# An expert layer that sends its results back to token order, instead of gathering them afterwards

## The reference

```python
x = x + gnn0(layernorm(x), adj)     # three gated graph layers (GRU)
x = x + ffn0(layernorm(x))          # 8 experts, the best 2 per token, relu
x = x + gnn1(layernorm(x), adj)     # relational graph layer, gated
x = x + ffn1(layernorm(x))          # norm again, 8 experts, best 2, gelu
```

## Time and profile before

| what | us |
|---|---|
| run, median of three | 1913.77 |
| profiled execution: span from first to last instruction | 1878.7 |
| TensorE, VectorE, ScalarE, GpSimd busy | 963.7, 984.4, 731.1, 683.2 |
| setup | 0 to 57.6 |
| first scatter phase | 478.5 to 667.7 |
| first expert phase | 667.7 to 934.7 |
| relational | 934.7 to 1248.0 |
| second scatter phase | 1274.0 to 1442.5 |
| second expert phase | 1442.5 to 1711.0 |
| combine | 1711.0 to 1878.7 |

### The profile page before, as it was taken

The page is one execution under the profiler, slowest core; times in us unless marked ns, Lnnn a source line. Parts: engine busy times, 40 slices in busy tenths (PEclk is TensorE's granted clock), DMA queues, the critical chain, the costliest instruction groups (busy, mean ns, idle before and its releaser), DMA issues. The chain is left out here.

```text
span 1878.7 us, 30179 instructions
## 1 busy us (share of the span) xinstructions
PE 963.7 (51%) x9146; PEld 626.6 (33%) x9147; DVE 984.4 (52%) x2604; ACT 731.1 (39%) x1231; POOL 683.2 (36%) x705
## 2 busy tenths in 40 slices
PE   1059999943230069999834535410001999993000
PEld 1034444422130047777612222210000777772000
DVE  4768788788630035555447777871000555652222
ACT  0158877843320046677512323210001776661000
POOL 1322222231677710000077656416774000004776
PEclk8579999965555589999955555555555999997555
DMA  9100000000541122222111111003111222222232
GB/s 315 59 1 1 1 0 0 0 1 0 167 172 52 49 66 79 79 82 84 60 44 35 30 28 32 15 1 133 52 52 55 76 82 78 78 78 62 75 80 74
DMA packets 71140, 114.00 MB, mean 61 GB/s; under 512 B 13078, under 2 KB 35474, under 8 KB 70804
## 3 DMA queue, kind: packets, MB, share of 16 engines
q1 hardware_dynamic: 41380, 67.21, 10.8%
q0 software_dynamic: 16384, 33.59, 6.0%
q10 hardware_dynamic: 13296, 12.33, 2.1%
HBM read 57.23 MB, written 55.92 MB: 60 GB/s over the span
## 5 line engine op out<-in xcount | busy, mean ns | idle before, releaser
L892 POOL DMA_INDIRECT slots<-ROWS,pos x256 | 266.1, 1040 | 109.1 <-issue 83.6
L1221 POOL DMA_INDIRECT d_G<-results,pos x128 | 121.9, 952 | 310.5 <-PEq L1569 271.8
L1165 ACT ACTIVATE e1hf<-bank,VT 128x512 f32<-128x512 f32 x156 | 105.2, 685 | 195.9 <-PE bank L331 195.9
L1188 DVE SCALAR_TENSOR_TENSOR e2hs<-e2hf,e2hs 128x512 f16<-128x512 f32 x156 | 104.1, 688 | 102.8 <-ACT e2hs L1170 102.8
L1188 DVE SCALAR_TENSOR_TENSOR e1hs<-e1hf,e1hs 128x512 f16<-128x512 f32 x156 | 104.1, 688 | 102.2 <-ACT e1hs L1170 102.2
L687 POOL TENSOR_TENSOR a_Z<-a_Z,a_H 128x512 f32<-128x512 f32 x48 | 61.1, 1273 | 219.6 <-ACT a_Z L584 219.6
L1221 POOL DMA_INDIRECT c_G<-results,pos x128 | 126.2, 986 | 35.9 <-issue 35.9
L1165 ACT ACTIVATE e2hf<-bank,VT 128x512 f32<-128x512 f32 x156 | 104.5, 685 | 75.0 <-PE bank L331 75.0
L1116 PE MATMUL bank<-ident,e2xs 128*128 128x128 f16 x312 | 24.2, 221 | 186.4 <-DMA e2xs<-slots 186.4
L1184 DVE COPY e2xT<-bank 128x1024 f16<-128x1024 f16 x39 | 26.7, 684 | 172.9 <-PE bank L1116 172.9
L329 PE MATMUL bank<-W,e1hs 128*128 x624 | 107.2, 220 | 0.0
(11 more groups left out here) (291 smaller groups left out, 3131.4 us busy)
## 6 DMA issues: line engine op xcount, KB each, us to landing
slots<-W ACTq DMA_DIRECT2D x78, 128.0 KB, 3.8
e1xs<-slots SPq DMA_DIRECT2D x39, 256.0 KB, 2.7
results<-e1ys SPq DMA_DIRECT2D x39, 256.0 KB, 2.0
e2xs<-slots SPq DMA_DIRECT2D x39, 256.0 KB, 2.7
results<-e2ys SPq DMA_DIRECT2D x39, 256.0 KB, 2.0
w_stage<-in_L_ffn_W_dram SPq DMA_DIRECT2D x2, 2048.0 KB, 12.7
slots<-ROWS,pos POOLq DMA_INDIRECT x256, 2.2
kept<-w_OUT SPq DMA_DIRECT2D x4, 1024.0 KB, 4.7
```

What stands on the lines that cost most here:

```text
L892: pool.indirect_dma_start(out=k["slots"], out_offset=bass.IndirectOffsetOnAxis(ap=k["pos"][:, c, t:t + 1], axis=0), in_=k["ROWS"][:, t, :] ...
L1165: act.activation(hf[c][:, :], HB[c][:, :], func, bias=VT[:, bass.ds(e * CH + b1_col + c, 1)], scale=1 / PS).then_inc(h_f32, 1)
L1188: dve.scalar_tensor_tensor(out=hs[j][:, 1, c, :], in0=hf[c][:, :], scalar=AS, in1=hs[j][:, 0, c, :], op0=ALU.mult, op1=ALU.subtract).then_ ...
L1221: pool.indirect_dma_start(out=dst, out_offset=None, in_=k["results"], in_offset=bass.IndirectOffsetOnAxis(ap=k["pos"][:, c, t:t + 1], axis ...
```

## The change

Each row in `slots` grows by four bytes of address and four of share, from 512 to 520 bytes. The address is the place of the result in token order: token number for the first choice, 8192 more for the second. Unused rows get an address beyond 16383. In the expert phase GpSimd scatters each block's results, four times 128 rows, by the address that stands in the row, with a bounds check that drops the unused ones; VectorE multiplies by the share as it copies out. `results` is then in token order, and `relational` and `combine` fetch it with plain loads on SyncE and add it unweighted. Along with it: two `slots` and two `results` buffers, one per expert layer; the filling of `slots` moves from ScalarE in setup to SyncE in the graph phase; the block ring is six rows deep, lies in `ROWS`, and a place is loaded again only when the block's results have been stored; the scatter of rows goes through all first choices, then all second ones, since the label in `ROWS` has to be rewritten in between; the output is stored from ScalarE's queue.

```diff
+XRING = 6
+ROW = 2 * P + 4
-        results = nc.dram_tensor("results", [NBLK * BLK, P], F32).ap()
+        results = [nc.dram_tensor(f"results{m}", [2 * TOK, P], F32).ap() for m in range(2)]
...
@@ setup, ScalarE
-            act.wait_ge(pchain, 1)
-            zrows = slots.rearrange("(n p r) c -> n p (r c)", p=P, r=2)
-            for n in range(zrows.shape[0]):
-                act.dma_start(zrows[n], zero).then_inc(zeroed, 16)
@@ gated_graph, SyncE
+            for slots in k["slots"]:
+                rows = slots.rearrange("(n p r) c -> n p (r c)", p=P, r=GT)
+                for n in range(k["NBLK"]):
+                    sp.dma_start(rows[n], flat(k["EMPTY"][:, :, :]).bitcast(I32)).then_inc(k["zeroed"], 16)
@@ labels and the scatter of rows
+def label_rows(dve, k, c, h, labelled):
+    NT = k["NT"]
+    part = slice(h * NT // 2, (h + 1) * NT // 2)
+    ids = k["ROWS32"][:, part, P:P + 1]
+    shares = k["ROWS32"][:, part, P + 1:P + 2].bitcast(F32)
+    one = lambda a: a.rearrange("p (t o) -> p t o", o=1)
+    dve.tensor_scalar(ids, one(k["dest"][:, part]), c * NT * P, None, ALU.add)
+    dve.tensor_copy(shares, one(k["prob"][:, c, part])).then_inc(labelled, 1)
...
+def send_rows(pool, k, slots, labelled, sent):
+    H = k["NT"] // 2
+    for c in range(2):
+        for h in range(2):
+            pool.wait_ge(labelled, 2 * c + h + 1)
+            for t in range(h * H, (h + 1) * H):
+                pool.indirect_dma_start(
+                    out=slots, out_offset=bass.IndirectOffsetOnAxis(ap=k["pos"][:, c, t:t + 1], axis=0),
+                    in_=k["ROWS32"][:, t, :], in_offset=None).then_inc(sent[h], 16)
...
@@ experts, SyncE and GpSimd
+            def step(b, j, i):
+                if not (isinstance(b, int) and b + XRING >= NBLK):
+                    sp.wait_ge(y_stored[j % RING], 16 * GT * (uses(j, i) + 1))
+                    load(b + XRING, j)
+        @block.gpsimd
+        def _(pool):
+            for b in range(NBLK):
+                pool.wait_ge(y_sb, b + 1)
+                for q in range(GT):
+                    pool.indirect_dma_start(
+                        out=k["results"][m],
+                        out_offset=bass.IndirectOffsetOnAxis(ap=xr[b % XRING][:, q, P:P + 1], axis=0),
+                        in_=ys[b % RING][:, q * P:(q + 1) * P], in_offset=None, bounds_check=2 * k["NT"] * P - 1,
+                        oob_is_err=False).then_inc(y_stored[b % RING], 16)
-                sp.dma_start(flat(y_rows[:, bass.ds(b, 1), :]), ys[j][:, :]).then_inc(y_stored[j], 16)
@@ experts, VectorE
-                dve.tensor_scalar(ys[j][:, :], YB[j][:, :], 1 / PS, None, ALU.mult).then_inc(y_sb, 1)
+                for q in range(GT):
+                    t = dve.tensor_scalar(ys[j % RING][:, q * P:(q + 1) * P], YB[j % RING][:, q * P:(q + 1) * P],
+                                          xr[j][:, q, P + 1:P + 2].bitcast(F32), 1 / PS, ALU.mult, ALU.mult)
+                t.then_inc(y_sb, 1)
@@ relational and combine
 def mix(dve, k, G, t0, sem_half, sem_full, n):
+    xg = flat(tiles_of(k["X"], t0, GT))
     for c, done in ((0, sem_half), (1, sem_full)):
-        for q in range(GT):
-            x = tile_of(k["X"], t0 + q)
-            i = dve.scalar_tensor_tensor(out=x, in0=G[c][:, q, :], scalar=k["prob"][:, c, bass.ds(t0 + q, 1)], in1=x,
-                                         op0=ALU.mult, op1=ALU.add)
+        dve.tensor_tensor(xg, xg, flat(G[:, c, :, :]), ALU.add).then_inc(done, 1)
-def gather(pool, k, t, c, dst, sem):
-    pool.indirect_dma_start(out=dst, out_offset=None, in_=k["results"],
-                            in_offset=bass.IndirectOffsetOnAxis(ap=k["pos"][:, c, t:t + 1], axis=0)).then_inc(sem, 16)
+def fetch(sp, k, m, g, G, sem):
+    rows = k["results"][m].rearrange("(c t p) d -> p c t d", c=2, p=P)
+    for c in range(2):
+        sp.dma_start(G[:, c, :, :], rows[:, c, bass.ds(GT * g, GT), :]).then_inc(sem, 16)
```

More of the change, by code:

```diff
@@ L127, in program @@
         phase(nc, route, locals(), "2")
[L128 removed]
+        phase(nc, scatter_reload, locals(), dma_sems[2:4])
         phase(nc, experts, locals(), "2", ACT.Gelu, C_B1B, 1)
@@ L905, in _ @@
         def _(pool):
-            send_rows(pool, k, sent)
+            send_rows(pool, k, k["slots"][1], labelled, sent)
+        @block.vector
+        def _(dve):
+            label_all(dve, k, labelled, sent)
         @block.sync
@@ L1019, in part @@
                 return dve.scalar_tensor_tensor(out=out, in0=src, scalar=WS, in1=first, op0=ALU.mult, op1=ALU.subtract)
+            for h in range(2):
+                label_rows(dve, k, 0, h, labelled)
             for n, step in enumerate((
@@ L1049, in _ @@
             dve.tensor_copy(k["general"][:, :], banks[1][:, 0:1])
+            for h in range(2):
+                dve.wait_ge(sent[h], 16 * (NT // 2))
+                label_rows(dve, k, 1, h, labelled)
 def experts(nc, k, tag, func, b1_col, m):
@@ L1065, in experts @@
         ring = range(RING)
-        xs = [sb(f"xs{j}", [P, GT, 2, P], F16) for j in ring]
+        six = range(XRING)
+        xr = [k["ROWS32"][:, GT * j:GT * (j + 1), :] for j in six]
+        xs = [k["ROWS"][:, GT * j:GT * (j + 1), :] for j in six]
         xT = [sb(f"xT{j}", [P, 2, BLK], F16) for j in ring]
@@ L1070, in experts @@
         ys = [sb(f"ys{j}", [P, BLK], F32) for j in ring]
-        x_loaded = [sem(f"x_loaded{j}") for j in ring]
+        x_loaded = [sem(f"x_loaded{j}") for j in six]
         y_stored = [sem(f"y_stored{j}") for j in ring]
@@ L1078, in rounds, with uses @@
         def rounds(eng, step):
-            for j in ring:
+            whole = NBLK // XRING - 1
+            for j in six:
                 step(j, j, 0)
-            with eng.Fori(1, NBLK // RING - 1) as i:
-                for j in ring:
-                    step(RING * i + j, j, i)
-            for j in ring:
-                step(NBLK - RING + j, j, NBLK // RING - 1)
+            with eng.Fori(1, whole) as i:
+                for j in six:
+                    step(XRING * i + j, j, i)
+            for b in range(whole * XRING, NBLK):
+                step(b, b % XRING, b // XRING)
+        def uses(j, i):
+            return XRING // RING * i + j // RING
         last = lambda b: isinstance(b, int) and b == NBLK - 1
@@ L1320, in _ @@
                 sp.dma_start(relrows[:, n * P:(n + 1) * P], ins["L1_gnn_" + name]).then_inc(rows_packed, 16)
+            for g in two:
+                fetch(sp, k, 0, g, G[g], gathered[g])
             sp.wait_ge(rows_packed, 64)
-            with if_general(sp):
-                def group(g):
+            for g in range(NG):
+                with if_general(sp):
                     def rel(r):
@@ L1328, in group @@
                     turns(sp, RELS, rel)
-                turns(sp, NG, group)
+                if g + 2 < NG:
+                    sp.wait_ge(full, g + 1)
+                    fetch(sp, k, 0, g + 2, G[g % 2], gathered[g % 2])
         @block.tensor
```

136 lines of the change are left out of this document (61 added, 75 removed).

## The result

The changed kernel takes 1852.37 us (median of four runs, 1843.04 to 1855.34) where the kernel before takes 1913.48 on the same chip: a ratio of 0.967, with a 95% interval of 0.965 to 0.970. It is faster by 61 us; 158 were forecast, and 1852 lies above the range (1730 to 1815).

What follows compares the result with a forecast made beforehand. GpSimd's gathers were taken to bound the combine, TensorE the experts, no engine the relational phase. Terms -122 - 33 - 17 + 1 + 12 + 1 = -158 gave a span of 1721, a run of 1756 us; range 1730 to 1815.

Steps and rivals of the forecast that it cites:

- Combine: Last phase: 128 gathers replaced by plain loads and stores, 167.7 us down to 46, -122 us; bounds 41 to 65.
- the stream: Combine: 12.6 MB of loads and stores at 305 GB/s take 41 us and are what is late next.
- Relational: Relational phase, 313.3 us: -33 us from shorter intervals between mixtures and an earlier first mixture; bounds -15 and -50.
- the third root: Relational phase: the third norm waits for GpSimd's root behind gathers, 16.3 us in 8 waits; ScalarE's gate becomes VectorE's largest wait.
- Setup: Setup phase: zeroing moves to SyncE in the graph phase, so it ends near 39.5 to 42.5 instead of 57.6, -17 us.
- sending the rows: Row-scatter phases: 128 scatters each as before, rows of 520 bytes instead of 512, plus short labelling instructions: +1 us.
- 35.1 us lie around the span and stay: Whole run: profiled span 1878.7 us against the runs' median 1913.8; the difference is added unchanged to the forecast span.
- Hidden: Expert phases: four scatters take GpSimd 5.4 us per block, inside TensorE's 6.46; only the ends cost, +6 per phase, +12.
- rival C: Experts: GpSimd keeps ports it took first, VectorE's two-input instructions wait, 8.3 us per block, +147 us, 1903; 2%.
- rival A: Experts: GpSimd's scatters become the bound; 1780 to 1860 us, taken at 1.8 us per scatter: +58, 1814; 19%.
- wrong altogether: Sign that the forecast fails: a combine above 80 us or an expert block above 7 us.
- Longer code +1: Expert loops: six blocks unrolled instead of three were put at +1 us.

Runs made afterwards that it cites:

- plain_again: The changed kernel with expert results stored by one plain transfer per block in block order, no scatters, on a chip where the kernel before takes 1912.25 us: 1694.95 us.
- after_loop3: The changed kernel with loop bodies and row ring of three blocks instead of six, addresses and shares copied to a table, scatters kept: 1722.04 us, ratio 0.915.
- before_loop6: The kernel before with six blocks instead of three in the loop's body of both expert phases: 1874.07 us, ratio 0.996.
- half_late: The changed kernel with two of four expert scatters per block, held back until TensorE has turned over the rows three blocks further on: 1709.80 us.
- loop3_again: Unchanged copy of after_loop3, run on a chip where the kernel before takes 1912.25 us: 1870.47 us.
- dropped: The changed kernel with a bounds check of 0 in the expert scatters, so nearly all rows are thrown away: 1838.62 us.
- gps_work: The changed kernel with plain stores instead of expert scatters, plus four power instructions over 128x4 on GpSimd per block: 1698.83 us.
- half: The changed kernel with only two of the four expert scatters per block, half of the results never stored: 1715.02 us.
- before_again2: The kernel before, unchanged, with a profile of its own on another chip: 1912.25 us.

## Why the prediction was wrong

**The bounds of the kernel and the phases outside the experts: right.** Combine: 42 us against 46, with the DMA engines full (share 1.04, 300 GB/s), so the stream was the bound as said; I had charged some microseconds too much for its ends. Relational: the wait for the third root (28.6 us in 15 waits over the whole phase) went to 4.6, and ScalarE's gate took its place as forecast:

```profile
DVE c_sg L1519 <- ACT c_sg L1465: 28.4, 14, 4.3
DVE X L1272 <- DMA c_G<-results: 21.2, 1, 21.2
DVE X L1272 <- issue: 9.3, 5, 2.4
...
DVE c_norm_c L359 <- POOL c_rs L353: 4.6, 11, 0.9
```

The last six intervals between mixtures are 17.9 and 13.9 in turn, 15.9 on the mean against the 15.8 of the sum. The 6 us more than forecast are at the start: the first six intervals take 81.3 us instead of 89, the first of them 6.5 instead of 12 or more. Setup ends at 41.0, and sending the rows costs nothing.

**"35.1 us lie around the span and stay": wrong.** About 2 us do (1.8 to 2.2 in the runs of both kernels). The profiled execution of before (1878.7) matches the 1881 chip, the median of its runs (1913.8) the 1913 chips, and the 32 us between them are the hole in the relational phase and VectorE's issue waits in the combine. On a 1913 chip the change therefore also takes away what the gathers cost there: combine 186.6 to 42 (-145), relational 326.4 to 273.9 (-53), setup -17, experts +145, with the rows -70 from a span of 1910.3: 1840, and 1841.2 was measured. The error of the constant hid part of the other one: with 2 us around the span the sum would have been 1723, 129 below the result and not 96. What I should have questioned was one line: a span and a median that differ by 2%, and that I bridged with a constant.

**"Hidden" in the experts, +12: wrong, by the size and by the mechanism.** GpSimd's side was sized well (5.6 us per block, idle at each block's end), rival C didn't occur (its 8.3 us per block should have been 8.1 by the earlier trace rows, 151.33 / 39 + 0.4 + 3.8), and neither did rival A: the 1852 lies between its 1780 and 1860, but by luck, since GpSimd never became the bound. The prediction's own sign for "wrong altogether", a block above 7 us, is what came. The step that failed is "5.4 us per block, hidden": I priced a scatter by what it costs GpSimd and what it might cost VectorE, and put what it does to TensorE at nothing. The runs show that four scatters per block take TensorE's block from 6.46 to 8.0 us and more on a 1913 chip, with issue gaps in its second product, and that plain stores in their place (plain_again) take it back. No row of the kernel before could show this, since nothing indexed ran beside the expert phase's TensorE. The first and last copy-out, the last scatter and the next phase's first transfer of the changed kernel show how the 70 us of the first phase divide:

```profile
669.48 1.13 DVE L1262 TENSOR_SCALAR e1ys<-bank,ROWS 128x128 f32<-128x128 f32 x4
...
973.67 1.12 DVE L1262 TENSOR_SCALAR e1ys<-bank,ROWS 128x128 f32<-128x128 f32 x4 [2.11 <-PE bank L331]
...
981.35 0.98 POOL L1157 DMA_INDIRECT results<-e1ys,ROWS  x1 [0.30 <-issue]
...
988.36 0.98 SPq L1362 DMA_DIRECT2D relrows<-in_L_gnn_b_fwd_dram  x1
```

38 intervals in 304.2 us are 8.0 us each, instead of 6.46: 59 us. The tail from the last copy-out's end (974.8) is 13.6 us instead of 2.9: the last eight scatters stand in a row, and the phase ends 6.0 us after the last, where I had counted 2.2 from its issue. That is +10.7 where I had said +6; on the 1881 chip (after_loop3) the tail is as long, 13.3 us.

**"Longer code +1": small, but of the other sign.** before_loop6 gives -3.5 per phase. I suspected it first, wrongly.

On the 1881 chip the same change, in the form of after_loop3, takes 1722 us with a span of 1720.4; the sum had said 1721. That it agrees to the microsecond is luck: the experts cost 22 us there (278.4 and 279.4 instead of 267.0 and 268.5), not 12, and the other phases give back as much more. The changed kernel itself was not run there. So the forecast would probably have been a good one on a chip like that of the profile, and the metric was taken on the other kind.

**What stays open.** Why two indexed transfers per block cost TensorE nothing and four cost 1.8 us. Two, issued after a copy-out, lie beside the end of the first product (12 matmuls in 2.6 us) and reach 0.8 us into the second (48 in 2.7 us); four reach further into it, which could explain the loss. But a threshold in their number would too, and half_late didn't meet a 1913 chip. That ScalarE and VectorE, which take few instructions, are held up in the kernel before, and that gaps come when GpSimd is idle, speak against any account in which TensorE's fast pace at the moment of a scatter is the whole cause. Open, too, are whether the instruction or its packets do it, and why chips differ in this.

## What to carry to other kernels

Before a profile and a set of times are put into one sum, compare the span with the runs: a constant of 2% around a span was here the sign that they came from different chips, and every term must then be asked which of the two it belongs to. An indexed transfer on GpSimd can have a price that isn't on GpSimd: look at the issue gaps of the engines beside it, TensorE with short matmuls above all, and measure it on more than one chip. And when a group of experiments says that each suspect alone is harmless, repeat one slow and one fast kernel on the same chip before forming a theory of their product.

## What the runs showed of the hardware

- On three chips of the experiments' four, other engines have issue gaps in phases with indexed transfers: 8.3 us (changed kernel) to 8.6 us (loop3_again) instead of 6.5 per expert block, VectorE down to one 128x128 instruction in 1.40 us during a combine, ScalarE over 10 us late once in a relational phase. The gaps also lie where GpSimd does nothing (the last 18 us of that combine's slow stretch). The bytes of the transfers aren't needed for it (dropped), arithmetic on GpSimd doesn't do it (gps_work), and two scatters per block instead of four don't either (half).
- In the stretches below, no code was loaded from DRAM beside these gaps. Between 760 and 840 us of the changed kernel TensorE had 11 us of issue gaps, and of the queues only two moved packets; q8 and q14, the instruction queues, have no line (nor in before_again2 between 965 and 985 us, the hole, or between 1806 and 1903, the slow combine):

```profile
DMA packets 2528, 4.80 MB, mean 60 GB/s; under 512 B 770, under 2 KB 772, under 8 KB 2528
...
q1 hardware_dynamic: 1296, 2.40, 11.1%
q0 software_dynamic: 1232, 2.40, 9.4%
```

- The Trainium skill, page "Runtime: NRT & Kernel Launch", section "Instruction fetch mechanics", has a long kernel streamed without having to fit the instruction memory, with fetching hidden behind dispatch, and a stall where a taken branch's target isn't in the current window and has to be fetched. The first agrees with before_loop6: a body twice as long, 7 us faster. The last isn't shown: between 700 and 900 us of the kernel before ten loop ends cost 0.5 us each, and only three packets moved on the instruction queues. The gaps beside scatters say nothing against the page, since no fetch is seen beside them.
- A scatter beside the expert phase's VectorE takes 1.09 us, against 0.96 in the second scatter phase, with the other engines idle.
- Where 32 loads and 16 stores of 256 KB stream at 300 GB/s, a load lands after 6.0 us instead of the 2.7 of the earlier trace rows.
